# Attention gathers without an index bound, padding that reads real rows, and 220 blocks in place of 224

## The reference, cut to what matters

```python
Q = (enh @ Wq + bq).reshape(N, H, D)          # N = 3125, H = 4, D = 64
K = (enh @ Wk + bk).reshape(N, H, D)
V = (enh @ Wv + bv).reshape(N, H, D)
mod_k = K[src] + 0.2 * rel[:, None, :]
scores = jnp.einsum('ehd,ehd->eh', Q[dst], mod_k) / D ** 0.5
...
ex = jnp.exp(scores - seg_max[dst])
denom = jax.ops.segment_sum(ex, dst, num_segments=N)
agg = jax.ops.segment_sum((ex / denom[dst])[:, :, None] * V[src], dst, num_segments=N)
```

## Time and profile before

| | |
|---|---|
| runs of the kernel before | 5474.56, 5459.92 and 5472.8 us |
| median | 5472.8 us |
| span of the profiled execution | 5466.2 us |
| time of the profiled execution outside its span | not given; the span stands 6.6 us under the median |
| busy in the span | PE 4441.3, DVE 3446.3, ACT 1954.9, POOL 3138.7 us |
| att_rows, first instruction to the next stage's first | 1734.8 to 2968.4 us |
| att_nodes | 2968.4 to 3357.6 us |

### The profile page before, as it was taken

How to read it: one execution, slowest core, us unless ns; L and a number is a source line. 1 busy time by engine, 2 the same in 40 slices (tenths; PEclk the granted TensorE clock), 3 DMA queues, 4 the chain that set the end, 5 groups by cost and what they waited for, 6 DMA issues and landing times. The chain is left out here.

```text
span 5466.2 us, 68774 instructions
## 1 busy us (share of the span) xinstructions
PE 4441.3 (81%) x20103; PEld 3234.6 (59%) x20103; DVE 3446.3 (63%) x6836; ACT 1954.9 (36%) x6195; POOL 3138.7 (57%) x2019
## 2 busy tenths in 40 slices
PE   6779679879866878788886887499848999998988
PEld 4557457657644666666665664355526777775455
DVE  7686576776667888888887787511165444443355
ACT  2332233333221656656665786122211221111122
POOL 2023588788788777777776887788443444440000
PEclk9999889989978888888888998599969999999999
DMA  9999623322324888888862444399835555552010
GB/s 301 303 345 335 167 33 41 60 35 39 71 17 105 248 248 246 246 239 241 239 200 66 72 96 115 75 268 297 252 126 188 203 204 193 199 197 68 0 29 24
DMA packets 767010, 878.82 MB, mean 161 GB/s; under 512 B 387191, under 2 KB 630168, under 8 KB 763364
## 3 DMA queue, kind: packets, MB, share of 16 engines
q1 hardware_dynamic: 334890, 620.50, 34.0%
q0 software_dynamic: 412656, 238.08, 21.0%
q10 hardware_dynamic: 19146, 16.44, 1.0%
HBM read 676.64 MB, written 226.45 MB: 165 GB/s over the span
## 5 line engine op out<-in xcount | busy, mean ns | idle before, releaser
L669 POOL DMA_INDIRECT pairs<-REC,FARC x800 | 1671.9, 2090 | 584.2 <-issue 226.4
L1034 PE MATMUL a_pa<-a_VW,identf 128*128 128x260 f32 x1792 | 576.2, 477 | 246.6 <-issue 154.7
L925 POOL DMA_INDIRECT a_KV<-kv_tab,KEYS x560 | 576.4, 1029 | 173.2 <-issue 159.5
L1034 PEld LDWEIGHTS a_pa<-a_VW,identf 128*128 128x128 f32 x1792 | 403.3, 236 | 331.8 <-issue 175.8
L2555 DVE TENSOR_TENSOR AIN<-AIN,w_pin 128x512 f32<-128x512 f32 (+1 forms) x325 | 216.4, 666 | 392.7 <-PE w_pin L2594 386.6
L997 ACT ACTIVATE a_VW<-a_KV,a_VW 128x64 f32<-128x64 f32 x1680 | 410.2, 334 | 2.7
L925 POOL DMA_INDIRECT XN<-kv_tab,KEYS x336 | 346.3, 1031 | 102.4 <-issue 92.4
L2489 POOL TENSOR_TENSOR RES<-RES,REC 128x1600 f32<-128x1600 f32 x52 | 185.3, 3582 | 252.5 <-DMA REC<-pairs 252.3
L2602 PE MATMUL w_pout<-FIO,w_tT 128*128 128x256 f32 x1250 | 321.3, 381 | 9.3 <-ACT w_tT L2570 9.3
L2570 ACT ACTIVATE w_tT<-w_pt 128x256 f32<-128x256 f32 (+1 forms) x325 | 118.7, 373 | 539.3 <-PE w_pt L2590 539.3
L2489 POOL TENSOR_TENSOR HB<-HB,REC 128x1600 f32<-128x1600 f32 x48 | 171.1, 3583 | 236.1 <-DMA REC<-pairs 236.0
(11 more groups left out here) (635 smaller groups left out, 10188.6 us busy)
## 6 DMA issues: line engine op xcount, KB each, us to landing
pairs<-ZERO SPq DMA_DIRECT2D x32, 5000.0 KB, 44.8
e_W<-in_L_ffn_w SPq DMA_DIRECT2D x192, 512.0 KB, 6.3
REC<-pairs SPq DMA_DIRECT2D x100, 800.0 KB, 8.3
RES<-pairs SPq DMA_DIRECT2D x13, 3200.0 KB, 10.2
HB<-pairs SPq DMA_DIRECT2D x12, 3200.0 KB, 10.5
m_crow<-cell_tab SPq DMA_DIRECT2D x73, 488.3 KB
row_tab<-a_arow SPq DMA_DIRECT2D x224, 130.0 KB, 3.9
n_AR<-row_tab SPq DMA_DIRECT2D x28, 1040.0 KB, 5.4
```

What stands on the lines that cost most here:

```text
L669: pool.indirect_dma_start(self.pairs[half], bass.IndirectOffsetOnAxis(self.FARC[:, i:i + 1].bitcast(I32), 0), self.REC[:, i, 0:4].bitcast( ...
L925: pool.indirect_dma_start(KV[t % UB][:, j, :], None, self.kv_tab, bass.IndirectOffsetOnAxis(self.SIDX[:, t * ROW + j:t * ROW + j + 1], 0), ...
L1034: last = pe.matmul(sums[t % NA], self.identf[:, :], VW[:, t % NV, e, :, :], start=e == 0, stop=e == ROW - 1)
```

## The change

The four gathers of a block lose their bound. A padding slot's index is clamped to 3125 + p / 2 for partition p, one of the rows 3125 to 3188 of `kv_tab`, which belong to no node but are written with finite numbers by project. A padding slot's row is now read and moved; its weight is still zero. The five memsets and their semaphore go. RB falls from 224 to 220, 112,640 slots, and with it every loop over blocks, the gathers among them (896 to 880). The last load of att_nodes is cut to the four blocks that are left.

```diff
-RB = 224
+RB = 220
...
+            spare = sb("spare", [P, 1])
...
+                    dve.tensor_scalar(spare[:, :], self.pcol[:, :], 0.5, float(N), ALU.mult, ALU.add)
...
                             dve.tensor_scalar(VB[:, :], SIDX[:, :, :].rearrange("r p b -> r (p b)"), N - 0.5, -BIG, ALU.is_gt, ALU.mult)
+                            dve.drain()
+                            dve.tensor_scalar(SIDX[:, :, :], SIDX[:, :, :], spare[:, :], None, ALU.min)
                             dve.drain()
                             dve.tensor_copy(self.SIDX[:, :], SIDX[:, :, :].rearrange("r p b -> r (p b)"))
...
-                        if t < OWN:
-                            pool.memset(KV[t], 0.0).then_inc(s_clr, 1)
-                            pool.wait_ge(s_clr, t + 1)
                         for j in range(ROW):
-                            pool.indirect_dma_start(KV[t % UB][:, j, :], None, self.kv_tab, bass.IndirectOffsetOnAxis(self.SIDX[:, t * ROW + j:t * ROW + j + 1], 0),
-                                                    bounds_check=N - 1, oob_is_err=False).then_inc(s_got[t % UB], 16)
+                            pool.indirect_dma_start(KV[t % UB][:, j, :], None, self.kv_tab, bass.IndirectOffsetOnAxis(self.SIDX[:, t * ROW + j:t * ROW + j + 1], 0)).then_inc(s_got[t % UB], 16)
...
-                            sp.dma_start(AR[:, r // UB, :, :], self.row_tab[ds(t * P, UB * P), :].rearrange("(t p) d -> p t d", p=P)).then_inc(s_ld[r // UB], 16)
+                            k = min(UB, RB - t)
+                            sp.dma_start(AR[:, r // UB, 0:k, :], self.row_tab[ds(t * P, k * P), :].rearrange("(t p) d -> p t d", p=P)).then_inc(s_ld[r // UB], 16)
```

More of the change, by code:

```diff
@@ L873, in att_rows @@
         NQ, NA, NV, NH = 4, 4, 4, 3
-        s_bc, s_clr = [n(f"a_bc{i}") for i in range(AHEAD)], n("a_clr")
+        s_bc = [n(f"a_bc{i}") for i in range(AHEAD)]
         s_got, s_out = self.soft_sems("a_got", UB), self.soft_sems("a_out", AU)
```

## The result

| | before | after |
|---|---|---|
| runs, us | 5474.56, 5459.92, 5472.8, 5469.79 | 5379.49, 5389.81, 5386.43, 5385.93 |
| median, us | 5471.3 | 5386.18 |
| ratio, 95% interval | | 0.9842 [0.983, 0.9853] |
| span of the profiled execution, us | 5466.2 | 5377.8 |
| attention rows, us | 1233.6 | 1152.3 |

The change is worth 85 us. That is inside the range of 5382 to 5438 and 17 us better than the 5403 predicted. A stage is counted from its first instruction to the first of the next. The profiled executions lie 88.4 us apart, and these are spread as follows: attention rows -81.3, attention nodes -9.5, the later stage of the expert gathers -7.2 (420.9 to 413.8), project +1.1, the unchanged work ahead of project's first matmul +8.7 (it comes at 1646.1 instead of 1637.4 us), everything else together within 0.3.

What follows compares the result with a forecast made beforehand. GpSimd's gather issue, 10.66 us a pair, was taken as the bound, with the other engines' loop just below. Attention rows -66.6, nodes -4.8 and project +1 sum to -70 us: 5403 from the 5472.8 median, range 5382 to 5438.

Steps and rivals of the forecast that it cites:

- GpSimd's issue sets the pace before: Attention rows, kernel before: GpSimd issues gathers back to back, 1.334 us each, 10.66 us a pair of blocks.
- The bound's price: Gathers on GpSimd: without the bound 0.946 us instead of 1.009, 63 ns saved; issue falls to 10.17 us a pair.
- The rival in which the bound costs nothing: Attention rows: unbounded gathers save nothing (1.018 us), issue stays at 10.66 us a pair, 5436 us in all; chance 0.16.
- The loop takes over: Attention rows: the TensorE and VectorE loop, without GpSimd, sets the pace at 10.2 to 10.5 us a pair, taken as 10.35.
- the rival with 5383: Attention rows: issue still sets the pace, fully freed, at 10.17 us a pair, 20 us more saved; chance 0.12.
- The opening: Start of attention rows: first pair ends 5.5 us earlier; 5 us added for TensorE's lower clock.
- Memsets: GpSimd, start of attention rows: dropping five memsets takes 11.9 us off GpSimd, partly before the first pair, the rest a lead.
- Two pairs less: Attention rows: 110 pairs of blocks in place of 112; two pairs are 21.3 us at the old pace.
- Padded slots hidden: End of attention rows: 12,640 padding slots move 2 KB each, 26 MB, hidden behind the loop at about 90% DMA.
- The rival of hot rows: Last 15.5 blocks of attention rows: padding reads of 64 rows served badly, about 5490 us when deciding; chance 0.06.
- The node stage: End of attention nodes: four blocks fewer on VectorE, at 2.38 us for two blocks, save 4.8 us.
- Project: Projection stage: the clamp, one more VectorE operation on 128x880 values, costs 1 us.

## Why the prediction was right or wrong

- **GpSimd's issue sets the pace before: right.** Cheaper gathers alone bring 41 us, a bound that drops nothing takes 49 us back, and the gather waits go and come with it.
- **The bound's price: right, a little less.** Predicted 63 ns a gather (1.009 to 0.946), measured 52 in the median (957) and 58 in the mean. Issue came to 10.22 us a pair, not 10.17. The rival in which the bound costs nothing is out: its 1.018 us did not occur.
- **The loop takes over: right as far as VectorE's waits show; its pace was the mis-sized term.** The loop term was "I take 10.35 us, between the two stretches". It measured 10.23, which is 109 x 0.12 = 13 us. Of the two stretches in the earlier trace rows, the one with 10.21 was the loop's own pace, and the one with 10.47 was not. The reason is that a gather wait leaves echoes in the pairs behind it. No run was made for it, but the pairs of the kernel before from 1800 to 2900 us, sorted by their distance from the last gather wait, show it: 11.54 us in the mean with such a wait (17 pairs), 11.39 for the next pair (13), 10.78 for the one behind that (11), and 10.28 for all later ones (61). The stretch with 10.47 began with the second pair behind a wait. How the echo runs through TensorE is argued: in the changed kernel TensorE pauses ahead of line 1034 for at most 2.5 us, against 6.3 before, and its granted clock rose from 0.87 to 0.90; the two other kernels that keep the bound stand at 0.86 in the same window.

The longest pauses of TensorE ahead of line 1034 (total, times, longest), in the changed kernel from 1800 to 2860 us, then in the kernel before from 1800 to 2900 us:

```profile
PE a_pa L1034 <- issue: 108.6, 64, 1.7
...
PE a_pa L1034 <- ACT a_VW L997: 83.7, 40, 2.5
```

```profile
PE a_pa L1034 <- issue: 147.9, 76, 6.3
```

- **Loop or issue: the rival with 5383 came nearest in time, but not by its mechanism.** The two paces lie less than 0.02 us apart. That VectorE waits for no gather after the opening says that the loop is the later of the two. So does the time from the end of a pair's last gather issue to that pair's line 983: in the changed kernel it is 14.1 us in the mean of pairs 8 to 19, while it is 15.4 and 15.8 us in the two unbounded kernels with memsets, at nearly the same pace (10.24 and 10.27 from the eighth pair on). If gathers held VectorE back, it would be the same in all three. GpSimd was expected to run ahead until it waits for buffers, and that was wrong: behind the opening this time hardly grows (14.4 us in the mean of the last dozen pairs), issue taking 10.230 and pairs 10.242 us. The surplus of the long gathers, 0.13 us a pair, is just what keeps issue from its bare 8 x (0.957 + 0.305) = 10.10, and every one of them lies beside an instruction of VectorE (below), so the two limits may not be independent. Whether this holds them in step stays open; fewer or slower gathers were not run at this pace.
- **The opening: wrong in both terms, and they nearly cancel.** The first pair's end came 2.5 us earlier, not 5.5: the late load of the third pair's types took the place of the wait for gathers. The 5 us added for TensorE's lower clock did not occur: the first eight intervals between pairs take 10.2 us already. Together with the pace this makes 13 + 5 - 3 = 15 us, which is the -81.3 that stands against the predicted -66.6. Why the types landed later is open: the third pair's compare came 11.4 to 12.1 us after the stage's start in three kernels with memsets, 15.1 and 14.4 in the two without, but also late in the one with the memsets put back.
- **Memsets: right in size, not in place.** 10.8 of the 11.9 us show. But the prediction put 5 of them ahead of the first pair and let the rest go into a lead; with the memsets put back, the first pair ends only 0.3 us later after the stage's start (24.1 against 23.8 us), and the other 10.5 us lie in the pairs behind it. They were in the sum all the same, since 1194.1 us, the stretch it started from, is 11 us more than 111 pairs of 10.66.
- **Two pairs less: right.** 21.5 of the 25 us of the row count alone.
- **Padded slots hidden: right**, at a DMA share of 0.86, not 0.90. The rival of hot rows did not happen with 64 rows. Its mechanism is real, though: with one row a gather cost 1.51 us of the DMA engines. At four gathers and the 1.18 us of the other queue a block would want 7.2 us where the loop gives 5.1, so on a chip like the first ones its 16 last blocks would cost some 34 us. That is an estimate, which takes the gather's cost to be the same there, and wasn't run.
- **The node stage: right in direction.** -9.5 against -4.8. Of the six kernels on the ordinary chips, those with 224 blocks took 388.1 and 389.2 us and those with 220 took 379.3 to 386.0, so four blocks are worth 2 to 10 us and the spread is as large as the effect.
- **Project: right.** +1.1 us.
- **Not foreseen and not explained:** -7.2 us in the expert stage and +8.7 ahead of project. No line of these changed. In two profiles of one and the same kernel (no one-hots) on two of the slower chips, these stretches differ by 9.1 and 9.7 us, so they are taken as chance, and they nearly cancel.
- **Long gathers: the reading of the earlier trace rows saw half of it.** In the changed kernel 77 of 837 gathers from 1800 to 2900 us took over 1.0 us. 26 of them overlap the one-hot compare of line 951, and the other 51 overlap line 967, VectorE's multiplication of one slot; none overlaps neither. What nearly all of them share is that VectorE's instruction is already running when the gather starts: line 967 began 0.08 to 0.41 us ahead in all 51, line 951 0.13 to 0.28 us ahead in 24 of the 26. On the slower chips 2 to 8 of some 600 gathers are over 1.0 us, all of them beside line 951, no gather at all meets the line that is 967 here, and without the one-hots none is long. GpSimd's timeline and VectorE's, one gather of each kind:

```profile
2397.23 1.16 POOL L926 DMA_INDIRECT XN<-kv_tab,KEYS  x1 [0.30 <-issue]
...
2403.75 1.14 POOL L926 DMA_INDIRECT a_KV<-kv_tab,KEYS  x1 [0.30 <-issue]
```

```profile
2396.81 0.74 DVE L967 TENSOR_TENSOR a_VW<-a_KV,a_VW 128x256 f32<-128x256 f32 x2
...
2403.59 0.48 DVE L951 TENSOR_SCALAR a_otT<-a_tyb,a_pc 128x1024 bf16<-128x1024 bf16 x1
```

## What to carry to other kernels

Read a limit that is about to take over from the stretches in which the present one is absent, and leave out the pairs right behind a wait: here the two behind it still carried its echo. When issue of indirect transfers is back to back, a bound on the index is worth clearing away even where nothing is dropped, by clamping the index once and letting padding read real, spread-out rows; but look first whether issue or landing sets the pace, since an engine that waits for landings has nothing to gain from cheaper issue.

## What the runs showed of the hardware that was not expected

- The index bound costs 52 ns of GpSimd a gather of 128 rows (1009 to 957 ns in the median) even when no index exceeds it. Whether padding rows are dropped or moved doesn't show in the issue time.
- The same program took about 5470 us on some chips and 5847 to 5880 on others. In the attention rows variants of the changed kernel moved 192 GB/s there at a mean DMA share of 0.67, where the changed kernel moved 263 at 0.86 on the first chips, and with a quarter of the gathers left out the ratio was 0.94 in place of 0.99.
- Many reads of one DRAM row are dear: 1.51 us of all 16 DMA engines for a gather of 128 times one 2 KB row, where with 64 rows, for about the same bytes, it was 0.458 x 80 / 46 = 0.80 us.
- A gather takes longer when VectorE's line 951 or 967 is already running as it starts: in the changed kernel this is so for at least 75 of the 77 gathers over 1.0 us, up to 1.37 us where the median is 0.957.
- A memset on GpSimd holds up a compare on VectorE. In the kernel before, VectorE's timeline and then GpSimd's show

```profile
1742.57 1.90 DVE L950 TENSOR_SCALAR a_ohT<-a_dlb,pcol 128x256 bf16<-128x256 bf16 x1 [1.64 <-DMA a_tyb<-ty_tab]
```

```profile
1742.56 1.83 POOL L922 MEMSET a_KV<- 128x2048 f32 x1
```

where the same compare takes 0.29 us with no memset beside it. By the rule of the Trainium skill (SBUF — State Buffer, "Who interferes with whom") that the two engines take a shared port pair in turns, a whole instruction each, this is what one would see, and the trace agrees here.
